# A selective-scan and expert layer on one core: a new lead-in for its first round, and its first rounds in an order written out

## Chip, cores and metric

One core of a Trainium2 chip. The time is device microseconds of one execution, the median of several runs.

## What is computed

x is 32 sequences of 256 tokens with 128 channels, fp32. First a state-space (Mamba) block on the normed x, added to x; then eight experts, two of them per token, on the normed sum, added again.

```python
xr = x @ W_in
xi, res = jnp.split(xr, 2, axis=-1)
u = silu(causal_conv4(xi) + conv_b)
dbc = u @ W_x                       # 8 columns for delta, 16 for B, 16 for C
delta = softplus(dbc_delta @ W_dt + b_dt)
h = exp(delta * A) * h + delta * B * u     # along the sequence, 256 channels x 16 states
y = (sum_n h * C + u * D) * silu(res)
x = x + y @ W_out
x = x + sum over the two best experts of p_e * (silu(n(x) @ w1[e].T) @ w2[e].T)
```

x in the first line and n(x) in the last are layer-normed over the channels.

## The kernel before

It works in 16 rounds of two sequences (512 tokens). Channels lie on partitions, so a [128, 2, 512] tile holds all 256 inner channels of a round. For each of 16 states a round has: a row of B spread over all partitions by TensorE (`row_b`, L1305, into one of two PSUM halves of `rows`), the product with `du` = delta·u on VectorE (`inputs`, L974), the decays exp(delta·A) on ScalarE (`decay`, L742), the scan on VectorE (`scan`, L984), the product with C on GpSimd (`outputs`, L471), and the sum over states as transposes that accumulate in PSUM (`sum_states`, L1326). `row_b(n)` waits for the scan of n-2, since there are two halves; `h` and `dA` are rings of eight states, so scan n waits for the sum of n-8.

Beside this, later rounds are prepared and earlier ones finished: norm (`norm_stats` L992, `inverse_deviation` L432 to L447 on GpSimd, `norm_apply` L634 on ScalarE), `turn_x`, `convolve` (L1246: the four taps times W_in as four matmuls per half, with `w_conv` made once by L1132), `conv_silu` L659, `project_bcd` L1265, `project_gate` L1256, then delta. The 8 delta columns and B must be more exact than one bf16 number: the projection is cut into high, middle and low bf16 parts (`high`, `middle`, `low`, with `take_high` and `take_middle` taking out what is already held), and `delta_rank` L1293 multiplies the parts by W_dt, split in the same way (`split_dt_weights`). softplus is relu(v) + ln(1 + exp(-|v|)): `soft_parts` L706 (abs) and L707 (relu), `soft_exponential` L715, `soft_log` L722; `add_soft` and `times_u` make `delta` and `du`. C goes through DRAM to be spread over the partitions (`store_c`, `load_c`). The experts are `hidden` (L1374, silu L776) and `expert` (L1384), weighted on VectorE (L1053) and added on GpSimd (L511).

Each engine's order is written out as one body `round_(i)` in which the parts of several rounds (i, i-1, ... i-6) are interleaved, and `run` issues it: the first bodies unrolled, the middle ones in a hardware loop, the last rounds as a list by hand. Parts of rounds that don't exist are left out, so the first bodies are the steady order with holes. Round 0's own preparation is the `lead_in` of each engine, ahead of `run`:

```python
def there(*js):
    return all(j.loop is not None or 0 <= j.at < rounds for j in js)
```

In `lead_in`, VectorE takes the statistics of round 0, copies `select`, makes `w_conv`, takes the statistics of round 1, splits W_dt and then waits for `soft_ready` to form `delta` (L1139) and `du` (L1142) of round 0. ScalarE applies the norm, copies `xnT`, does both silus, `skip`, `high`, `copy_bcd`, `middle`, `low` with the two gate silus between them, and softplus. TensorE first runs 40 transposes of the identity (L1524), then the products in that order, both gate projections and the first two rows of B. `w_bc` is filled by ten small transfers on ScalarE's queue.

## Time and profile before

| | |
|---|---|
| median of 3 runs (lowest, highest) | 1105.02 us (1104.96, 1106.01) |
| profiled execution, its span | 1103.15 us, 1101.2 us |
| TensorE (PE) busy | 1037.8 us, 94% |
| VectorE (DVE) busy | 1012.7 us, 92% |
| ScalarE (ACT) busy | 908.2 us, 82% |
| GpSimd (POOL) busy | 960.5 us, 87% |
| transfers | 76 GB/s over the span |

PEld is TensorE's weight load, which runs beside its matmuls. Times of rows are counted from the start of the span. A row of waits reads "who waited <- for whom". The granted clock of TensorE is given as a share of 2.4 GHz; it has two levels, 1.2 and 2.4 GHz.

### The profile page before, as it was taken

What the parts mean: (1) busy time and instruction counts of PE and PEld (TensorE: products, weight loads), DVE (VectorE), ACT (ScalarE), POOL (GpSimd) and SP (SyncE); (2) the same over time, 40 slices, a digit from 0 to 9 for tenths busy, and PEclk for the clock granted to TensorE, in tenths of its full rate; (3) what the DMA queues carried; (4) which work ended last, traced back from release to release, by engine and by line L of the source; (5) the groups of instructions that cost most, each with busy time, mean ns of one, the idle gap of its engine ahead of it and who ended that gap; (6) DMA issues with size and microseconds to landing.
All of it is one profiled execution on the core that took longest, in us unless ns stands there. A gap on an engine that the chain in (4) does not pass through costs nothing.

```text
span 1101.2 us, 18699 instructions
## 1 busy us (share of the span) xinstructions
PE 1037.8 (94%) x6152; PEld 759.1 (69%) x6152; DVE 1012.7 (92%) x1038; ACT 908.2 (82%) x1382; POOL 960.5 (87%) x892
## 2 busy tenths in 40 slices
PE   7558679999999999999999999999999999989997
PEld 4336457777777777767777777777777776767775
DVE  2799999999999999999999999999999999999721
ACT  4967578988999899899989999899989989875533
POOL 3388698998999999999999999999999999799834
PEclk9798889999999999999999999999999999989999
DMA  5321313104031311303131220403130120320000
GB/s 152 157 86 49 116 58 116 59 28 155 2 126 58 126 59 68 115 0 138 44 125 57 91 91 7 172 2 125 57 135 39 68 105 0 136 87 10 11 10 10
DMA packets 39760, 84.03 MB, mean 76 GB/s; under 512 B 5744, under 2 KB 30624, under 8 KB 31392
## 3 DMA queue, kind: packets, MB, share of 16 engines
q1 hardware_dynamic: 36848, 83.05, 21.0%
q10 hardware_dynamic: 2864, 0.38, 0.2%
q8 instruction: 25, 0.41, 0.2%
q14 instruction: 23, 0.19, 0.1%
HBM read 78.70 MB, written 4.72 MB: 76 GB/s over the span
## 4 chain that ended last, share of the span: by engine, by line
PE 84%; DVE 6%; ACT 4%; issue 3%; POOL 1%; DMA 0%; POOLq 0%; ACTq 0%; DVEq 0%
PE work L1384 19%; PE work L1374 18%; PE y_ps L1326 17%; PE work L1246 9%; PE rows L1305 4%; DVE h L984 4%; PE work L1265 3%; PE work L1347 3%; PE work L1230 2%; PE rows L1384 2%; PE work L1256 2%; PE rows L1374 1%; DVE rows L974 1%; PE work L1293 1%; ACT dA L742 1%
## 5 line engine op out<-in xcount | busy, mean ns | idle before, releaser
L471 POOL TENSOR_TENSOR h<-h,c_rows 128x1024 f32<-128x1024 f32 x256 | 600.4, 2367 | 75.1 <-DVE h L984 75.0
L984 DVE TENSOR_TENSOR_SCAN h<-dA,rows 128x1024 f32<-128x1024 f32 x256 | 579.4, 2276 | 1.9 <-ACT dA L742 0.7
L742 ACT ACTIVATE dA<-delta,a_neg 128x510 f32<-128x510 f32 x512 | 325.4, 708 | 1.7 <-POOL delta L455 0.5
L974 DVE TENSOR_TENSOR rows<-du,rows 128x1024 f32<-128x1024 f32 x256 | 307.1, 1213 | 3.7 <-PE rows L1305 3.6
L1326 PEld LDWEIGHTS y_ps<-ident,h 128*128 128x128 f32 x2048 | 242.6, 145 | 52.2 <-issue 36.3
L1326 PE MATMUL y_ps<-ident,h 128*128 128x128 f32 x2048 | 267.5, 278 | 2.6 <-POOL h L471 2.6
L1384 PEld LDWEIGHTS work<-w,hid 128*128 128x128 f32 x1856 | 223.2, 193 | 36.5 <-ACT hid L776 20.8
L1374 PE MATMUL work<-x2T,w 128*128 128x512 f32 x474 | 238.3, 597 | 0.3
L1384 PE MATMUL work<-w,hid 128*128 128x128 f32 x1856 | 229.0, 277 | 3.5 <-ACT hid L776 3.2
L776 ACT ACTIVATE hid<-work 128x512 f32<-128x512 f32 x237 | 139.2, 596 | 58.7 <-PE work L1374 56.8
L511 POOL TENSOR_TENSOR x<-x,weighted 128x512 f32<-128x512 f32 x128 | 163.4, 1277 | 23.4 <-DVE weighted L1053 23.0
L1305 PE MATMUL rows<-parts,select 96*128 96x512 bf16 x256 | 98.7, 387 | 32.1 <-DVE h L984 32.1
L1374 PEld LDWEIGHTS work<-x2T,w 128*128 128x128 f32 x474 | 81.9, 190 | 54.2 <-ACT hid L776 16.8
L1246 PE MATMUL work<-xnT,w_conv 128*128 128x512 f32 x256 | 116.5, 598 | 2.3 <-ACT xnT L651 1.5
L625 ACT ACT_TABLE_LOAD x73 | 93.7, 1283 | 1.3
L776 ACT ACT_TABLE_LOAD x56 | 71.8, 1283 | 22.5 <-PE work L1374 14.5
L1053 DVE TENSOR_TENSOR weighted<-work,cw 128x512 f32<-128x512 f32 x116 | 78.4, 676 | 9.3 <-PE work L1384 7.5
L1246 PEld LDWEIGHTS work<-xnT,w_conv 128*128 128x128 f32 x256 | 47.6, 191 | 51.8 <-issue 50.2
L1305 PEld LDWEIGHTS rows<-parts,select 96*128 96x128 bf16 x256 | 25.2, 99 | 65.1 <-DVE h L984 40.4
L1053 DVE TENSOR_TENSOR weighted<-rows,cw 128x512 f32<-128x512 f32 x12 | 8.2, 691 | 32.3 <-PE rows L1384 20.5
L462 POOL TENSOR_TENSOR du<-delta,u 128x1024 f32<-128x1024 f32 x15 | 35.5, 2364 | 1.8 <-POOL delta L455 1.3
L455 POOL TENSOR_TENSOR delta<-du,soft 128x1024 f32<-128x1024 f32 x15 | 35.5, 2366 | 0.0
(118 smaller groups left out, 953.9 us busy)
## 6 DMA issues: line engine op xcount, KB each, us to landing
c_rows<-c_dram SPq DMA_DIRECT2D x64, 1024.0 KB, 5.2
x_in<-in_x SPq DMA_DIRECT2D x16, 256.0 KB, 2.9
x_again<-in_x SPq DMA_DIRECT2D x16, 256.0 KB, 3.2
out<-x SPq DMA_DIRECT2D x16, 256.0 KB, 2.6
w<-in_w1T SPq DMA_DIRECT2D x1, 1024.0 KB, 6.3
w<-in_w2T SPq DMA_DIRECT2D x1, 1024.0 KB, 8.4
h<-in_conv_w SPq DMA_DIRECT2D x1, 512.0 KB, 4.9
c_dram<-bcd SPq DMA_DIRECT2D x16, 32.0 KB, 1.6
```

What stands on the lines that cost most here:

```text
L471: nc.gpsimd.tensor_tensor(at, at, c_rows[:, n, :].unsqueeze(1).broadcast_to([P, H, T]), ALU.mult).then_inc(c_used, 1)
L511: nc.gpsimd.tensor_tensor(x1[:, j.odd], x1[:, j.odd], weighted[:, e % 2], ALU.add).then_inc(expert_added, 1)
L625: nc.scalar.preload_act_table_set("natural_log_exp_and_others")
L742: last = nc.scalar.activation(two_seqs(dA[:, n % RING, half, :])[:, :, 1:], two_seqs(delta[:, half, :])[:, :, 1:], ACT.Exp, scale=a_neg[:, ...
L776: nc.scalar.activation(hid[:, e % 2, f, :], bank(place(HIDDEN, j, e, f)), ACT.Silu).then_inc(hid_ready, 1)
L974: nc.vector.tensor_tensor(rows[:, n % 2], du[:, j.odd], rows[:, n % 2, H - 1, :].unsqueeze(1).broadcast_to([P, H, T]), ALU.mult).then_inc( ...
L984: nc.vector.tensor_tensor_scan(h[:, n % RING].rearrange("p h t -> p (h t)"), dA[:, n % RING].rearrange("p h t -> p (h t)"), rows[:, n % 2] ...
L1246: last = nc.tensor.matmul(two_seqs(work[:, CONV[half], :]), w_conv[:, k, half * P:(half + 1) * P], xnT[:, :, k:k + SEQ], start=(k == 0), s ...
L1305: nc.tensor.matmul(rows[:, n % 2, H - 1, :], select[:, n, :], parts[:, j.odd, :], start=True, stop=True).then_inc(b_ready, 1)
L1326: last = nc.tensor.matmul(y_ps[:, half, b, :], h[:, n % RING, half, b * P:(b + 1) * P], ident[:, :], is_transpose=True, start=False, stop= ...
L1374: nc.tensor.matmul(bank(place(HIDDEN, j, e, f)), w1[:, e, f, :], x2T[:, j.odd, :], start=True, stop=True).then_inc(hid_projected, 1)
L1384: last = nc.tensor.matmul(token_bank(place(EXPERT, j, e))[:, b, :], hid[:, e % 2, f, b * P:(b + 1) * P], w2[:, f, e, :], start=(f == 0), s ...
```

## The change

It rewrites the lead-in of round 0 and writes out the first rounds of every engine, in place of the holed bodies:

- the first norm: VectorE aggregates and adds eps, GpSimd takes only the power, and the four 128-token blocks of `xn` are shared, two by ScalarE and two by VectorE;
- `w_conv` is made in two halves, one on VectorE, one on GpSimd;
- W_x comes with one transfer into a spare slot of `h`, and GpSimd copies its columns to their places in `w_bc` (seven copies);
- the projection of round 0 goes to another bank, starts with half 0 of `u`, and is copied whole as fp32 to `bcd`; delta's rank product is one fp32 matmul per half from these raw rows and W_dt as it is (`w_dt_first`), ahead of `high`, `middle` and `low`, which go on for B;
- softplus by halves, with the relus on VectorE; `delta` and `du` by halves;
- the gate projection, its silus and `skip` of round 0 move out of the lead-in into the first rounds;
- 27 instead of 40 transposes ahead of the first product;
- one small activation at the start loads the silu table early;
- `run` gets the index at which it begins: bodies up to 4 (TensorE, ScalarE, GpSimd), 5 (VectorE) and 6 (SyncE) are replaced by lists. The loop and the last rounds are the same.

```diff
@@ constants, helpers @@
-        WARM = 40
+        WARM = 27
+        spare = h[:, RING - 3].rearrange("p h t -> p (h t)")
+        w_dt_first = spare[0:SPLIT, 0:H * P]
+        w_x = spare[:, H * P:H * (P + RANK + 2 * NS)].rearrange("p (h n) -> p h n", h=H)
...
+            engine.tensor_tensor(w_conv[:, :, at], w_in[:, at].unsqueeze(1).broadcast_to([P, TAPS, P]),
+                                 taps_rows.rearrange("p (d k) -> p k d", k=TAPS)[:, :, at],
+                                 ALU.mult).then_inc(w_conv_ready, 1)
@@ sync @@
+                sp.wait_ge(w_dt_first_clear, 1)
+                sp.dma_start(w_dt_first[DT_ROWS[0]:DT_ROWS[0] + RANK, :], W_dt).then_inc(w_dt_first_loaded, 16)
+                fetch_x(Round(1))
                 sp.wait_ge(dt_rows_clear, 1)
...
-                fetch_x(Round(1))
...
+            sp.wait_ge(lead_norm, 1)
...
+            load_again(r[0])
+            load_again(r[1])
+            load_x(r[3])
+            load_x(r[4])
+            store_c(r[1])
+            load_c(r[1], 0)
+            load_c(r[1], 1)
+            load_x(r[5])
+            load_c(r[1], 2)
...
+            run(sp, round_, 7, 7, 19)
@@ gpsimd @@
+            pool.wait_ge(w_x_loaded, 16)
+            for half in range(H):
+                part_rows = w_bc[:, half, 0:3 * SPLIT].rearrange("p (a r) -> p a r", a=3)
+                for row, src in ((0, w_x[:, half, RANK:RANK + NS]),) + tuple(
+                        (row, w_x[:, half, 0:RANK]) for row in DT_ROWS):
+                    width = src.shape[-1]
+                    nc.gpsimd.tensor_copy(part_rows[:, :, row:row + width],
+                                          src.unsqueeze(1).broadcast_to([P, 3, width])).then_inc(w_bc_ready, 1)
+            nc.gpsimd.tensor_copy(w_bc[:, :, C_ROW:ROWS], w_x[:, :, RANK + NS:]).then_inc(w_bc_ready, 1)
+            pool.wait_ge(variance_ready[0], 1)
+            nc.gpsimd.tensor_tensor(rstd[:, 0, :], variance[:, 0, :], power[:, 0:TB],
+                                    ALU.pow).then_inc(variance_ready[0], 1)
+            pool.wait_ge(taps_loaded, 16 * TAP_LOADS)
+            weigh_taps(nc.gpsimd, 1)
...
+            inverse_deviation(r[1], 0)
+            inverse_deviation(r[2], 0)
+            outputs(r[0], 0)
+            outputs(r[0], 1)
+            outputs(r[0], 2)
+            outputs(r[0], 3)
+            outputs(r[0], 4)
+            outputs(r[0], 5)
+            inverse_deviation(r[3], 0)
...
@@ scalar @@
             act.dma_start(w_in[:, :], W_in).then_inc(taps_loaded, 16)
-            for part in range(3):
-                load(w_bc[:, :, part * SPLIT:part * SPLIT + NS],
-                     W_x[:, RANK:RANK + NS].rearrange("(h p) n -> p h n", p=P))
-            for part in range(3):
-                for row in DT_ROWS:
-                    load(w_bc[:, :, part * SPLIT + row:part * SPLIT + row + RANK],
-                         W_x[:, 0:RANK].rearrange("(h p) n -> p h n", p=P))
-            load(w_bc[:, :, C_ROW:ROWS], W_x[:, RANK + NS:RANK + 2 * NS].rearrange("(h p) n -> p h n", p=P))
...
-                pre_norm(lead)
+                act.wait_ge(constants_ready, CONSTANTS)
+                nc.scalar.activation(warm[:, :], one[:, :], ACT.Silu).then_inc(tables_warm, 1)
+                tables[0] = "silu"
+                act.wait_ge(rstd_ready[0], 1)
+                for b in range(TB // 2):
+                    last = nc.scalar.activation(xn[:, 0, b, :], x_in[:, 0, b, :], ACT.Identity,
+                                                bias=shift[:, 0, b:b + 1], scale=rstd[:, 0, b:b + 1])
+                last.then_inc(xn_ready[0], 1)
                 copy_xnT(lead)
                 act.wait_ge(weights_loaded, 16 * LOADS)
-                act.wait_ge(constants_ready, CONSTANTS)
                 for half in range(H):
                     conv_silu(lead, half)
-                skip(lead)
-                high(lead)
-                copy_bcd(lead)
-                middle(lead)
-                gate_silu(lead, 0)
-                low(lead)
-                gate_silu(lead, 1)
                 exp_tables()
-                for half in range(H):
-                    soft_parts(lead, half)
-                soft_exponential(lead)
-                soft_log(lead)
+                act.wait_ge(bcd_projected, 1)
+                nc.scalar.activation(bcd[0:ROWS, :], bcd_bank(lead)[0:ROWS], ACT.Copy).then_inc(bcd_ready, 1)
                 nc.scalar.activation(a_neg[:, :, :], a_neg[:, :, :], ACT.Exp).then_inc(a_ready, 1)
                 act.wait_ge(a_ready, 1)
                 nc.scalar.activation(a_neg[:, :, :], a_neg[:, :, :], ACT.Copy, scale=-1.0).then_inc(a_ready, 1)
                 act.wait_ge(a_ready, 2)
+                for half in range(H):
+                    act.wait_ge(dt_projected, half + 1)
+                    nc.scalar.activation(soft[:, half, :], bank(LEAD_DT[half]), ACT.Abs,
+                                         bias=dt_bias[:, half:half + 1]).then_inc(lead_abs, 1)
+                    act.wait_ge(lead_abs, half + 1)
+                    nc.scalar.activation(soft[:, half, :], soft[:, half, :], ACT.Exp,
...
+            skip(r[0])
+            decay(r[0], 0)
+            decay(r[0], 1)
+            pre_norm(r[1])
...
@@ vector @@
+            def first_norm():
+                pre_stats(r[0])
+                dve.wait_ge(stats_ready[0], 1)
+                for b in range(TB):
+                    last = nc.vector.bn_aggr(mean_variance[:, b, :], stats[:, 0, b, :])
+                last.then_inc(moments_ready[0], 3)
+                dve.wait_ge(moments_ready[0], 3)
+                nc.vector.tensor_scalar(variance[:, 0, :], mean_variance[:, :, 1], EPS, None,
+                                        ALU.add).then_inc(variance_ready[0], 1)
+                dve.wait_ge(taps_loaded, 16 * TAP_LOADS)
+                weigh_taps(nc.vector, 0)
+                dve.wait_ge(variance_ready[0], 2)
+                nc.vector.scalar_tensor_tensor(shift[:, 0, :], mean_variance[:, :, 0], -1.0, rstd[:, 0, :], ALU.mult,
+                                               ALU.mult).then_inc(rstd_ready[0], 1)
+                dve.wait_ge(rstd_ready[0], 1)
+                for b in range(TB // 2, TB):
+                    last = nc.vector.tensor_scalar(xn[:, 0, b, :], x_in[:, 0, b, :], rstd[:, 0, b:b + 1],
+                                                   shift[:, 0, b:b + 1], ALU.mult, ALU.add)
+                last.then_inc(lead_norm, 1)
+            def first_delta():
+                dve.wait_ge(weights_loaded, 16 * LOADS)
+                dve.wait_ge(bcd_ready, 1)
+                nc.vector.tensor_copy(parts[:, 0, :], bcd_bank(lead)[0:3 * SPLIT]).then_inc(high_ready, 1)
+                for half in range(H):
+                    dve.wait_ge(lead_abs, half + 1)
+                    nc.vector.tensor_scalar(du[:, 0, half, :], bank(LEAD_DT[half]), dt_bias[:, half:half + 1], 0.0,
+                                            ALU.add, ALU.max).then_inc(dt_read, 1)
+                dve.wait_ge(dt_read, H)
+                dve.wait_ge(u_ready, H)
+                for half in range(H):
+                    dve.wait_ge((lead_log, soft_ready)[half], 1)
+                    nc.vector.tensor_tensor(delta[:, half, :], du[:, 0, half, :], soft[:, half, :],
+                                            ALU.add).then_inc((lead_delta, delta_ready)[half], 1)
+                    dve.wait_ge((lead_delta, delta_ready)[half], 1)
+                    last = nc.vector.tensor_tensor(du[:, 0, half, :], delta[:, half, :], u[:, 0, half, :], ALU.mult)
+                last.then_inc(du_ready, 1)
-                pre_stats(r[0])
+                first_norm()
+                split_dt_weights()
+                pre_stats(r[1])
...
-                dve.wait_ge(rstd_ready[0], 1)
-                dve.wait_ge(taps_loaded, 16 * TAP_LOADS)
-                nc.vector.tensor_tensor(w_conv[:, :, :], w_in[:, 0:H * P].unsqueeze(1).broadcast_to(
-                    [P, TAPS, H * P]), taps_rows.rearrange("p (d k) -> p k d", k=TAPS),
-                    ALU.mult).then_inc(w_conv_ready, 1)
-                dve.wait_ge(w_conv_ready, 1)
-                pre_stats(r[1])
-                split_dt_weights()
-                dve.wait_ge(soft_ready, 1)
-                nc.vector.tensor_tensor(delta[:, :, :], du[:, 0], soft[:, :, :], ALU.add).then_inc(delta_ready, 1)
-                dve.wait_ge(delta_ready, 1)
-                dve.wait_ge(u_ready, H)
-                nc.vector.tensor_tensor(du[:, 0], delta[:, :, :], u[:, 0], ALU.mult).then_inc(du_ready, 1)
+                dve.wait_ge(w_conv_ready, H)
+                dve.wait_ge(w_bc_ready, COPIES)
+                first_delta()
+            inputs(r[0], 0)
+            inputs(r[0], 1)
+            next_pre_stats(r[2])
+            scan(r[0], 0)
+            scan(r[0], 1)
+            inputs(r[0], 2)
+            inputs(r[0], 3)
...
@@ tensor @@
                     nc.tensor.transpose(y_ps[:, 0, 0, :], ident[:, :], ident[:, :])
+                pe.wait_ge(lead_norm, 1)
                 turn_x(lead)
-                pe.wait_ge(w_conv_ready, 1)
+                pe.wait_ge(w_conv_ready, H)
                 for half in range(H):
                     convolve(lead, half, *([use_u(lead, 0)] if half and CONV[0] == CONV[1] else []))
-                pe.wait_ge(weights_loaded, 16 * LOADS)
-                project_bcd(lead)
-                project_gate(lead, 0)
+                pe.wait_ge(w_bc_ready, COPIES)
+                for half in range(H):
+                    pe.wait_ge(u_ready, half + 1)
+                    last = nc.tensor.matmul(bcd_bank(lead), w_bc[:, half, :], u[:, 0, half, :], start=(half == 0),
+                                            stop=(half == H - 1))
+                last.then_inc(bcd_projected, 1)
+                pe.wait_ge(w_dt_first_loaded, 16)
+                pe.wait_ge(bcd_ready, 1)
+                for half in range(H):
+                    nc.tensor.matmul(bank(LEAD_DT[half]), w_dt_first[:, half * P:(half + 1) * P], bcd[0:SPLIT, :],
+                                     start=True, stop=True).then_inc(dt_projected, 1)
                 take_high(lead)
-                project_gate(lead, 1)
                 take_middle(lead)
-                for half in range(H):
-                    delta_rank(lead, half, *([use_dt(lead, 0)] if half and DT[0] == DT[1] else []))
+                pe.wait_ge(dt_weights_ready, 2)
                 pe.wait_ge(select_ready, 1)
-                row_b(lead, 0)
-                row_b(lead, 1)
                 pe.wait_ge(dt_read, H)
             lead_in()
+            row_b(r[0], 0)
+            project_gate(r[0], 0, use_u(r[0], 0))
+            row_b(r[0], 1)
...
+            project_gate(r[0], 1, use_gate(r[0], 0))
+            turn_x(r[1], use_u(r[0], 1))
+            row_b(r[0], 6)
+            convolve(r[1], 0, use_gate(r[0], 1))
+            row_b(r[0], 7)
+            sum_states(r[0], 4)
+            row_b(r[0], 8)
+            sum_states(r[0], 5)
...
```

How the lists stand. **VectorE, from its statistics of round 0 to the first scan work, before:** (`BN_STATS` are the statistics, `COPY select` the rows that spread B)

```order
L1128 COPY select<-one_hot 96x2048 [waits one_hot_ready]
L1132 TENSOR_TENSOR w_conv<-w_in,h 128x1024 [waits taps_loaded,rstd_ready0]
L992 BN_STATS stats<-x_in 128x6 [waits rstd_ready0,x_loaded1,w_conv_ready]
...
L1122 TENSOR_TENSOR w_dt<-w_dt_part 96x256 [waits dt_weights_step]
L1139 TENSOR_TENSOR delta<-du,soft 128x1024 [waits soft_ready,dt_weights_ready]
L1142 TENSOR_TENSOR du<-delta,u 128x1024 [waits u_ready,delta_ready]
L992 BN_STATS stats<-x_in 128x6 [waits rstd_ready0,x_loaded0]
L992 BN_STATS stats<-x_in 128x6 x3
L974 TENSOR_TENSOR rows<-du,rows 128x1024 [waits b_ready,du_ready]
L984 SCALAR_TENSOR_TENSOR h<-dA,rows 128x1024 [waits dA_ready,b_made]
```

**and now:**

```order
L1391 BN_AGGR mean_variance<-stats 128x2 [waits stats_ready0]
L1394 TENSOR_SCALAR variance<-mean_variance 128x4 [waits moments_ready0]
L323 TENSOR_TENSOR w_conv<-w_in,h 128x4x128 [waits taps_loaded]
L1399 SCALAR_TENSOR_TENSOR shift<-mean_variance,rstd 128x4 [waits variance_ready0]
L1403 TENSOR_SCALAR xn<-x_in,rstd,shift 128x128 [waits rstd_ready0]
...
L1431 COPY select<-one_hot 96x2048 [waits one_hot_ready]
L1411 CAST parts<-rows 96x512 [waits weights_loaded,bcd_ready,w_bc_ready,w_conv_ready]
L1414 TENSOR_SCALAR du<-rows,dt_bias 128x512 [waits lead_abs] x2
L1420 TENSOR_TENSOR delta<-du,soft 128x512 [waits lead_log,u_ready,dt_read]
L1423 TENSOR_TENSOR du<-delta,u 128x512 [waits lead_delta]
L1420 TENSOR_TENSOR delta<-du,soft 128x512 [waits soft_ready]
L1423 TENSOR_TENSOR du<-delta,u 128x512 [waits delta_ready]
```

The norm's arithmetic is on VectorE, the copy of `select` and the split of W_dt stand behind it, and `delta` and `du` are made in halves.

**TensorE, from the first work of round 1 to row 7 of B of round 0, before:** (`rows<-parts,select` is a row of B, `ident,h` the sum over a state, `xnT,w_conv` a convolution half)

```order
L1230 MATMUL work<-ident,xn 128x128 [waits dt_read,xn_ready0]
...
L1246 MATMUL work<-xnT,w_conv 128x512 [waits dt_read,xnT_ready]
...
L1246 MATMUL work<-xnT,w_conv 128x512 [waits xnT_ready]
...
L1305 MATMUL rows<-parts,select 128x512 [waits scan_done] x3
L1315 MATMUL y_ps<-ident,ud 128x128 [waits skip_ready]
...
L1326 MATMUL y_ps<-ident,h 128x128 [waits c_used]
...
L1305 MATMUL rows<-parts,select 128x512 [waits scan_done] x3
L1265 MATMUL work<-u,w_bc 128x512 [waits u_ready]
```

**and now** (`xnT,w_in` is a half of the gate projection, `ident,xn` the turn of round 1):

```order
L1702 MATMUL rows<-parts,select 128x512 [waits dt_read,low_ready,select_ready,dt_weights_ready]
L1657 MATMUL work<-xnT,w_in 128x512 [waits u_ready,xnT_ready]
L1702 MATMUL rows<-parts,select 128x512
L1712 MATMUL y_ps<-ident,ud 128x128 [waits skip_ready]
...
L1702 MATMUL rows<-parts,select 128x512 [waits scan_done] x2
L1723 MATMUL y_ps<-ident,h 128x128 [waits c_used]
...
L1657 MATMUL work<-xnT,w_in 128x512 [waits gate_ready,xnT_ready]
L1631 MATMUL work<-ident,xn 128x128 [waits u_ready,xn_ready0]
...
L1702 MATMUL rows<-parts,select 128x512 [waits scan_done]
L1647 MATMUL work<-xnT,w_conv 128x512 [waits gate_ready,xnT_ready]
...
L1702 MATMUL rows<-parts,select 128x512 [waits scan_done]
L1723 MATMUL y_ps<-ident,h 128x128 [waits c_used]
...
L1647 MATMUL work<-xnT,w_conv 128x512 [waits xnT_ready]
```

From the third row of B on, the rows of round 0 stood behind both convolution halves of round 1; now seven rows stand ahead of the first half, and two between the halves.

## Rows read from the trace of the kernel before

**Rows 1.** The page's costliest groups: busy us, mean ns | idle before.
```profile
L984 DVE TENSOR_TENSOR_SCAN h<-dA,rows 128x1024 f32<-128x1024 f32 x256 | 579.4, 2276 | 1.9 <-ACT dA L742 0.7
...
L974 DVE TENSOR_TENSOR rows<-du,rows 128x1024 f32<-128x1024 f32 x256 | 307.1, 1213 | 3.7 <-PE rows L1305 3.6
```

**Rows 2.** Stretches: from:to length, busy by engine, PE clock, DMA.
```profile
36.00:60.00 24.00, 16.01 (x56) 9.74 (x57) 21.36 (x14) 19.20 (x29) 13.01 (x15) 0.85 0.09 31
60.00:120.00 60.00, 43.03 (x209) 29.46 (x209) 59.90 (x41) 40.25 (x61) 49.75 (x31) 0.86 0.17 62
120.00:182.57 62.57, 51.03 (x294) 37.17 (x292) 59.92 (x60) 51.57 (x80) 51.43 (x48) 0.92 0.25 83
182.57:247.23 64.66, 63.17 (x384) 46.20 (x384) 62.89 (x65) 57.48 (x88) 59.88 (x55) 1.00 0.21 76
...
311.04:373.81 62.77, 62.77 (x384) 46.35 (x384) 62.55 (x65) 57.49 (x88) 59.58 (x54) 1.00 0.22 79
```

**Rows 3.** DVE's waits from 36 to 247: total us, times, longest.
```profile
DVE rows L974 <- PE rows L1305: 2.2, 2, 1.8
DVE weighted L1053 <- PE work L1384: 2.0, 2, 1.0
DVE x L1024 <- PE work L1347: 1.4, 1, 1.4
DVE h L984 <- ACT dA L742: 0.7, 1, 0.7
```

**Rows 4.** Timeline of the lead-in: start us, us, engine [idle before].
```profile
4.62 0.87 DVE L992 BATCH_NORM_STATS2 stats<-x_in 128x6 f32<-128x128 f32 x4 [4.62 <-DMA x_in<-in_x]
...
8.47 1.04 POOL L444 TENSOR_TENSOR rstd<-variance,power 128x4 f32<-128x4 f32 x1
...
9.83 2.01 DVE L1132 TENSOR_TENSOR w_conv<-w_in,h 128x1024 f32<-128x1024 f32 x1 [3.21 <-POOL shift L447]
9.83 1.65 ACT L634 ACTIVATE xn<-x_in,shift,rstd 128x128 f32<-128x128 f32 x4 [2.08 <-POOL shift L447]
...
12.97 7.11 PE L1246 MATMUL work<-xnT,w_conv 128*128 128x512 f32 x16 [0.78 <-ACT xnT L651]
...
20.94 1.96 PE L1265 MATMUL work<-u,w_bc 128*128 128x512 f32 x4 [0.87 <-ACT u L659]
...
26.83 1.28 ACT L625 ACT_TABLE_LOAD   x1
...
28.12 0.69 ACT L706 ACTIVATE soft<-work,dt_bias 128x512 f32<-128x512 f32 x1
...
30.58 1.06 ACT L715 ACTIVATE soft<-soft 128x1024 f32<-128x1024 f32 x1
...
34.09 1.23 DVE L1142 TENSOR_TENSOR du<-delta,u 128x1024 f32<-128x1024 f32 x1
...
36.66 8.58 PE L1246 MATMUL work<-xnT,w_conv 128*128 128x512 f32 x16 [0.69 <-ACT xnT L651]
```

**Rows 5.** The same timeline, POOL beside DVE.
```profile
5.41 1.20 DVE L1128 COPY select<-one_hot 96x2048 bf16<-96x2048 bf16 x1
5.65 1.03 POOL L432 TENSOR_TENSOR moments<-stats 128x4 f32<-128x4 f32 x1 [1.73 <-DVE stats L992]
...
12.97 0.42 DVE L1113 TENSOR_TENSOR h<-h,w_dt_part 96x256 f32<-96x256 f32 x1
12.98 0.47 POOL L433 TENSOR_TENSOR moments<-stats 128x4 f32<-128x4 f32 x1
```

**Rows 6.** POOL's groups by line: busy us, mean ns | idle.
```profile
L511 POOL TENSOR_TENSOR x<-x,weighted 128x512 f32<-128x512 f32 x128 | 163.4, 1277 | 23.4 <-DVE weighted L1053 23.0
...
L504 POOL TENSOR_TENSOR cw<-picked 128x32 f32<-128x32 f32 x16 | 4.0, 253 | 1.3
```

**Rows 7.** DMA issues up to 60 us: KB, us to landing.
```profile
w_bc<-in_W_x ACTq DMA_DIRECT2D x4, 16.0 KB, 5.0
```

**Rows 8.** One more stretch, 36 to 158 us.
```profile
36.00:158.00 122.00, 87.84 (x413) 59.51 (x414) 117.61 (x97) 88.59 (x136) 93.20 (x68) 0.86 0.21 76
```

More of the change, by code:

```diff
@@ L424, in inverse_deviation @@
             def inverse_deviation(j, k):
-                if not there(j):
+                if not there(j) or (k == 0 and j.led()):
                     return
@@ L1297, in row_b @@
             def row_b(j, n):
-                if not there(j) or (n < 2 and j.led()):
+                if not there(j):
                     return
```

559 lines of the change are left out of this document (530 added, 29 removed).

## Prediction

> **What bounds the kernel now.** I read the costliest groups of the page first: VectorE (DVE) runs 256 scans of 2.28 us and 256 products of 1.21 us, 886.5 us of its work [rows 1]. The table of stretches then shows who sets a round's length: from 311.04 to 373.81 us, one full round, PE works 62.77 us of 62.77 and DVE 62.55 [rows 2]. TensorE (PE) and DVE both do. A round can't get shorter unless both get less to do, and the change leaves the full rounds alone. What can go is the time before the full rounds, and a microsecond won there moves all that follows: PE's remaining queue from the fourth loop body on is the same, and it has no idle time in which to lose the gain.
>
> That time has two parts. The **lead-in**: DVE writes `du` of round 0 at 34.09 for 1.23 us, so the first scan work can't begin before 35.32 [rows 4]. The **first rounds**: from 36 to 247.23 us DVE is busy 21.36, 59.90, 59.92 and 62.89 us of 24.00, 60.00, 62.57 and 64.66, which leaves 7.2 us idle [rows 2]. PE is busy only 16.01 + 43.03 of the first 84 us there. The list of waits names 6.3 of the 7.2 us: 2.2 for rows of B (PE's product stood behind both convolutions of round 1), 2.0 for experts of round 0, 1.4 for the first output projection, 0.7 for the first decays [rows 3]. No row names POOL.
>
> **The change, step by step (lead-in).**
> 1. *Norm.* DVE's statistics end at 5.49 [rows 4]. Today ten small POOL instructions follow and ScalarE (ACT) starts on `xn` at 9.83, for 1.65 us. Now DVE aggregates (4 short instructions, bounded by the 0.87 us of the four statistics; I take 0.4) and adds eps: about 6.3. POOL has to finish seven copies for `w_bc` before its power. Their source is one transfer issued at about 1.2; the nearest row needs 5.0 us to land [rows 7], so 6.2, or about 5 if it comes as soon as `x_in`, issued half a microsecond earlier and used at 4.62 [rows 4]. Seven copies at 0.25 each, as the 128x32 row [rows 6], are 1.8. I take 8.1 for the power's start (7.0 to 9.0), and 9.15 for its end (1.04, [rows 4]).
> 2. *A shared port.* The select copy on DVE ran 5.41 to 6.61, and POOL's first small instruction beside it took 1.03 us where its like take 0.2; at 12.98 another took 0.47 beside a DVE subtraction that ran to 13.39 [rows 5]. POOL waited for DVE both times. The change puts POOL's half of `w_conv` right behind the power, and DVE's `shift`, a tiny product of two SBUF operands, becomes ready at that moment. That DVE waits for POOL no row shows: 0 at one end; at the other the whole half, between 1.28 us (the 128x512 POOL sum, [rows 6]) and 2.1 (times 1.64, as DVE's `w_conv` ran 2.01 us against 1.23 for `du`). I take 0.6, less than half, since it is a race. So `shift` is there at about 10.05.
> 3. The Trainium skill (SBUF — State Buffer, section "SBUF: two separate sides") calls this pair of ports an exclusive lock: whichever instruction starts first keeps it, the other blocks for its whole length. By that the wait would be all or nothing, and the sum 0.6 us better or up to 1.5 worse; the two stretched POOL instructions agree with it for one direction.
> 4. *ACT half of `xn`*: 2 of 4 instructions, 0.9 instead of 1.65: ends 11.0 against 11.48. Turn, copy and start of the convolution then take 1.49 as today (11.48 to 12.97): it starts at 12.5. The select copy and the `dt` split leave this path for idle DVE time; if that idle time went, they would cost 1.2 + 3.3.
> 5. *Convolution and B, C*: 7.1, then silu of the second half 0.7, but the first half's product with `w_bc` already runs beside it: half of 1.96, and 0.3 of hand-over: ends at 21.6; today 22.90. The exp table load (1.28) now runs beside this, from 20.35 to 21.65, and the two gate silus (1.2) and the silu table's need for a swap at 26.83 leave the path.
> 6. *dt*: one copy to 22.25, two fp32 products (0.98 each, the first ready at 23.3), no wait for high, middle and low parts. ACT then does abs 0.69, exp, abs, exp, middle, ln, ln on 128x512 pieces. The halves of a 1.06 us exp are 0.53; with the fixed part seen in the 128x512 abs I take 0.65. First ln at 27.3, second at 27.9. The relus go to DVE beside it.
> 7. DVE: four half products of 0.64 from 27.3, the last pair after the second ln: `du` at 29.9. The low part is done at 28.5 and the row of B by 29, so they hide under it, with 1 us of cover.
>
> **Lead-in: 35.32 − 29.9 = 5.4 us gained** (3.3 to 7). The statistics of round 2 move from before the first product to behind it, which is no gain; three later ones move forward, which is no loss by 247 us.
>
> **First rounds.** The 7.2 us of idle DVE are an upper bound for what the explicit order can return. The removed waits have places: B rows 2 and 3 go ahead of everything of round 1; the convolutions stand between rows 6/7 and 8/9; the hidden products of round 0 start four rows of B earlier, which gives PE four more DVE steps for work that fills 63.17 of the last 64.66 us of this part today [rows 2]. What is late next: row 7 of B stands behind convolution half 0, half of 7.11, against a scan, a product and a scan on DVE, 5.8, before DVE needs it [rows 1]; at full clock it fits, at 1.2 GHz (twice as long) it is 1.7 us late with its neighbours, and a pair after a wait took 8.58 instead of 7.11 [rows 4]: 0 to 2 us, I take 1. The gate of round 0 now costs PE two products and ACT two silus and two table loads (3.8 us) inside round 0; ACT is busy 40.25 of the 60 us there [rows 2], so nothing; without that room round 1's parts come 3.8 late. POOL's sum and product for `du` of round 1 end when DVE reaches round 1, today without a wait that rows 3 names; 0.5. The first gating and residual sum, both earlier: 0.5. On SP, the stores and loads of C for round 1 stand behind two loads of x that wait for norms of rounds 1 and 2; those end before the C of round 1 is computed, since its convolution needs the first of them: nothing, and if they are late POOL's outputs wait, with eight states of `h` as cover. **7.2 − 2.0 = 5.2 us gained** (2 to 7.2).
>
> **Sum**: 10.6 us. The profiled execution took 1103.15 us, so 1092.5; the median of the runs shown is 1.87 above it, so **1094.4 us**. A measurement of this kernel can tell about 0.2% (2.2 us) from no change.
>
> **Rivals** (times against the median).
> - *B, everything returns*: no new waits and an early `shift`: 6.5 + 7 = 13.5, 1091.5. For it: PE is idle a third of the first rounds. Against: `du` of round 1 comes with no spare time. 0.15.
> - *C, only the lead-in*: the explicit order trades its 7.2 us of waits for others of the same size. For it: from 36 to 120 us the PE clock is granted at 0.85 and 0.86 of full speed [rows 2], so work that fits at full clock may not. 1099.6. 0.17.
> - *D, the port lock in full*: POOL's half goes first and takes 2.1 us: 1.5 more than in the sum, 1095.9. It is the page's rule above; rows 5 bear out one direction. 0.15.
> - *E, no change*: the change doesn't do what it says. The first row of B still waits for all split parts and the split `dt` weights; round 1's `du` still goes through POOL. If either chain is some 8 to 10 us late, all is given back: 1104. Against: DVE reaches the split by 11 us and has until 28.5 for it. 0.04.
> - *F, slower: TensorE at its lower clock*. From 36 to 158 us PE is busy 87.84 us of 122.00 at a mean granted clock of 0.86 [rows 8]: 28% of it at 1.2 GHz, the rest at 2.4. With busy time spread evenly that is 75.5 us of work at full clock. The new order puts nearly every product of rounds 0 and 1 behind a wait for a scan. If the part s of the work runs at 1.2 GHz it takes 75.5(1+s); it limits DVE (117.61 busy) from s = 0.56, and loses to today's 122 + 5.4 from s = 0.69; at 0.8 it takes 136, that is 8.5 us slower, 1113.5. Against: s was about 0.28 with the same waits, and PE's amount of work per DVE step hardly moves. 0.03. The Trainium skill (TensorE: Matmul & The Clock Gate, "HAM oscillation — how this bites in real kernels") warns of just this, matmul groups split by waits that each start cold; the 8.58 us row agrees for one group.
>
> **Chances.** The forecast has 0.46; its own range is 1091.5 to 1097.5. With the fast end of B and most of C, the range is **1090.5 to 1100.0**; outside lie E, F and tails. Faster by over 0.2%: 0.93; within: 0.04; slower: 0.03.
>
> **What the profile would show.** First product of DVE at 28.5 to 31.5 instead of 36.01; POOL's power over by 10; the convolution starting between 11.5 and 13.5; `shift` right behind the power, or only behind POOL's half (D). DVE idle from its first product to the fifth loop body 1 to 4 us instead of 7.2, waiting for B rows near the first convolution of round 1. Granted clock near 0.85 to that point. Full rounds of 62.8 us as before. Wrong would be: DVE idle for `du` of round 1, a PE mean clock near 0.6, or full rounds that grow.

## The result, and the profile after

The changed kernel takes 1099.36 us (median of 4 runs, 1098.39 to 1100.40) against 1104.99 for the kernel before in the same comparison: ratio 0.9944, 95% interval 0.9929 to 0.9959. That is 5.6 us less, where 10.6 were forecast. The profiled execution took 1100.40 us with a span of 1098.4; before it was 1103.15 and 1101.2. Between the two profiles lie only 2.75 us, and the first thing to do is to say where those are.

Table of stretches of the changed kernel, from VectorE's first product to the start of the fifth loop body (its third output projection), then two full rounds, then the next one. Columns as in [rows 2].
```profile
32.30:243.00 210.70, 179.22 (x944) 124.17 (x943) 204.26 (x180) 173.61 (x263) 173.83 (x146) 0.90 0.22 77
243.00:369.60 126.60, 125.95 (x766) 92.48 (x765) 125.33 (x129) 115.05 (x175) 118.60 (x108) 1.00 0.22 79
369.60:433.30 63.70, 63.05 (x384) 46.19 (x382) 62.70 (x65) 57.86 (x89) 60.93 (x56) 1.00 0.23 83
```
Before, the same stretches run from 36.01 to 247.10 (211.09 us, DVE busy 203.91), to 373.70 (126.60), and to 436.80 (63.10). So the first product is 3.7 us earlier, the fifth body 4.1 us, and the seventh still 4.1. Then gain is lost: the round from 369.60 takes 63.70 instead of 63.10, with PE busy 63.05 against 63.01. The sixteenth output projection starts at 1048.3 against 1051.1: 2.8 us are left.

Timeline of the changed kernel's lead-in: start, us, engine [idle before].
```profile
8.21 1.03 POOL L478 TENSOR_TENSOR rstd<-variance,power 128x4 f32<-128x4 f32 x1
9.23 1.51 POOL L323 TENSOR_TENSOR w_conv<-w_in,h 128x512 f32<-128x512 f32 x1
9.28 1.48 DVE L1399 SCALAR_TENSOR_TENSOR shift<-mean_variance,rstd 128x4 f32<-128x4 f32 x1 [2.02 <-POOL rstd L478]
...
11.81 0.63 PE L1631 MATMUL work<-ident,xn 128*128 128x128 f32 x4 [4.09 <-ACT xn L952]
...
13.22 8.62 PE L1647 MATMUL work<-xnT,w_conv 128*128 128x512 f32 x16 [0.78 <-ACT xnT L766]
...
32.30 2.36 DVE L1235 TENSOR_TENSOR rows<-du,rows 128x1024 f32<-128x1024 f32 x2
```
The norm is on time (power from 8.21, forecast 8.1). Then `shift`, a 4-column product, takes 1.48 us: it ends with GpSimd's half of `w_conv`. TensorE, idle for 4.09 us before the turn of `xn`, then needs 8.62 us for the convolution instead of 7.11 [rows 4]. The granted clock over it is 0.82, so part of it ran at 1.2 GHz; before it was 1.00. The stretches of the two convolutions, first the changed kernel's, then the one before (columns as in [rows 2]):
```profile
13.22:21.84 8.62, 8.62 (x17) 3.90 (x18) 3.26 (x10) 0.69 (x1) 3.64 (x10) 0.82 0.25 89
```
```profile
12.97:20.08 7.11, 7.10 (x16) 2.90 (x16) 2.80 (x9) 1.97 (x2) 3.33 (x10) 1.00 0.41 156
```

What VectorE waited for between 32 and 243 us (total, times, longest):
```profile
DVE rows L1235 <- PE rows L1702: 2.9, 4, 1.4
DVE weighted L1314 <- PE work L1781: 1.5, 2, 1.0
DVE yT L1276 <- PE work L1631: 1.2, 1, 1.2
DVE x L1285 <- PE work L1744: 0.2, 1, 0.2
```
The waits for decays, output projection and experts of [rows 3] are gone or smaller, and new ones stand in their place: `yT` for the turned y of round 0 (1.20), and for rows of B 2.9 us in all instead of 2.2, the longest for row 13 of round 1 behind the second convolution half of round 3 (1.39). Idle in all: 6.4 us against 7.2.

ScalarE's timeline in the round that grew, 416 to 425 us:
```profile
416.74 1.28 ACT L740 ACT_TABLE_LOAD   x1
418.03 1.95 ACT L856 ACTIVATE dA<-delta,a_neg 128x510 f32<-128x510 f32 x3
421.21 1.94 ACT L856 ACTIVATE dA<-delta,a_neg 128x510 f32<-128x510 f32 x3 [1.23 <-issue]
423.17 1.28 ACT L890 ACT_TABLE_LOAD   x1
```
The same place in the kernel before:
```profile
420.81 1.28 ACT L625 ACT_TABLE_LOAD   x1
422.11 3.78 ACT L742 ACTIVATE dA<-delta,a_neg 128x510 f32<-128x510 f32 x6
426.57 1.28 ACT L776 ACT_TABLE_LOAD   x1 [0.68 <-PE work L1384]
```
Six decays ran in one piece before; now ScalarE stops for 1.23 us between the two halves of one state, where the program has no wait. Before, ScalarE even had 0.68 us to spare behind them. It stops behind the same activation three times more, until 547.54 (for 0.97), 673.82 (0.99) and 799.85 (0.75). The place can be read from the program: the loop's body ends with `decay(one, 7)` and begins with `decay(two, 8)`, so the third activation of the row at 418.03 is the first of a new pass. The loop holds two rounds and runs five passes; the four stops stand one activation behind its four returns to the start, and there is none where it is entered or left. TensorE then waits for `hid`:
```profile
425.12 2.05 PE L1781 MATMUL work<-w,hid 128*128 128x128 f32 x16 [0.66 <-ACT hid L890]
```
The list of DMA queues names a candidate. From 430 to 830 us the changed kernel has the row below; the kernel before has no instruction queue in that stretch at all.
```profile
q14 instruction: 15, 0.12, 0.1%
```
Over the whole execution it is 43 packets against 23.

### The profile page after: what moved, and what is told of

Its sections match the earlier page's. It is cut to its first block, busy times and chain, and to the rows that moved or that the text cites. A ratio compares the mean times of both kernels' runs of the same rounds, so it can differ in the third digit from the quotient of the medians.

```text
span 1098.4 us, 18682 instructions
## 1 busy us (share of the span) xinstructions
PE 1042.4 (95%) x6139; PEld 758.1 (69%) x6139; DVE 1016.4 (93%) x1051; ACT 907.8 (83%) x1381; POOL 961.4 (88%) x892
## 4 chain that ended last, share of the span: by engine, by line
PE 74%; DVE 8%; issue 7%; ACT 6%; POOL 4%; DMA 0%; POOLq 0%; ACTq 0%; DVEq 0%
PE work L1781 17%; PE work L1771 16%; PE y_ps L1723 16%; PE work L1647 8%; DVE h L1245 6%; PE rows L1702 4%; PE work L1744 2%; ACT dA L856 2%; PE work L1631 2%; PE work L1666 2%; PE rows L1781 2%; POOL h L535 2%; PE work L1657 2%; PE rows L1771 1%; DVE rows L1235 1%
## 5 line engine op out<-in xcount | busy, mean ns | idle before, releaser
L1723 PE MATMUL y_ps<-ident,h 128*128 128x128 f32 x2048 | 270.8, 279 | 10.9 <-POOL h L535 10.9
L774 ACT ACTIVATE u<-work,conv_bias 128x512 f32<-128x512 f32 x32 | 22.0, 687 | 16.5 <-PE work L1647 16.3
```

Of the source, the lines that this page charges most:

```text
L1723: last = nc.tensor.matmul(y_ps[:, half, b, :], h[:, n % RING, half, b * P:(b + 1) * P], ident[:, :], is_transpose=True, start=False, stop= ...
```

## Experiments

Three theories for the missing five microseconds: the **port** (GpSimd holds up VectorE's `shift`), the **cold start** (TensorE partly at 1.2 GHz in the first convolution, since it had idled), and **code** (ScalarE's loop is loaded anew in each pass, since its place in the program has moved). Their common rival is that the first rounds have a limit of their own and swallow whatever the lead-in gains. First product, fifth body and idle VectorE between them are read from each profile; "full rounds" is from the third to the fourteenth output projection, eleven rounds.

| kernel | us, ratio to before (95%) | first product | fifth body | idle DVE | full rounds |
|---|---|---|---|---|---|
| before (profile) | 1103.15 | 36.01 | 247.1 | 7.2 | 694.1 |
| changed | 1099.36, 0.9944 (0.9929 to 0.9959) | 32.30 | 243.0 | 6.4 | 695.5 |
| e1_port | 1099.12, 0.9938 (0.9925 to 0.9950) | 32.15 | 242.8 | 6.5 | 695.9 |
| e2_warm | 1098.07, 0.9930 (0.9917 to 0.9943) | 32.46 | 240.5 | 4.3 | 695.7 |
| e3_pad | 1098.17, 0.9931 (0.9919 to 0.9944) | 33.89 | 242.6 | 5.0 | 694.2 |
| e4_three | 1095.83, 0.9911 (0.9898 to 0.9925) | 30.52 | 240.8 | 6.4 | 694.3 |
| e8_pad6 | 1099.25, 0.9936 (0.9922 to 0.9949) | 33.98 | 242.5 | 4.7 | 694.2 |
| h1_old_lead_new_order | 1102.73, 0.9974 (0.9965 to 0.9982) | 37.11 | 247.4 | 6.2 | 694.1 |
| h2_new_lead_old_order | 1109.04, 1.0035 (1.0022 to 1.0048) | 34.08 | 252.6 | 14.5 | 694.1 |
| e5_after_shift | 1097.54, 0.9934 (0.9921 to 0.9947) | 32.05 | 240.1 | 4.3 | 694.1 |
| e6_order | 1096.68, 0.9919 (0.9907 to 0.9932) | 33.65 | 241.3 | 3.9 | 694.2 |
| e7_all | 1094.32, 0.9892 (0.9877 to 0.9907) | 29.74 | 237.2 | 3.7 | 694.2 |
| before_again | 1103.12 (one) | 36.08 | 247.1 | 7.1 | 694.1 |
| before_warm46 | 1106.07, 0.9998 (0.9988 to 1.0008) | 36.07 | 248.9 | 8.9 | 694.1 |

Below the changed kernel (before: 1104.99) the medians belong to four comparisons, in which the kernel before took 1105.92, 1105.86, 1106.99 and 1105.77; so kernels of different comparisons are compared by their ratios.

**e1_port**
```diff
-            pool.wait_ge(taps_loaded, 16 * TAP_LOADS)
-            weigh_taps(nc.gpsimd, 1)
                 weigh_taps(nc.vector, 0)
+                weigh_taps(nc.vector, 1)
```


> The changed kernel, but VectorE makes both halves of w_conv while it waits for the power anyway, and GpSimd makes none. Port theory (VectorE's shift took 1.48 us because GpSimd's half of w_conv held the shared port from 9.23 to 10.74): shift takes about 0.2 us and is there at 9.5 instead of 10.76, xn and the convolution start 1.3 us earlier (near 11.9 instead of 13.22), the first product of VectorE comes 1.0 to 1.3 us earlier, and the time falls by about that, 1098.1. Rival (shift waited for the result of the power or for something else, as a semaphore that arrives late): shift stays at 1.4 us and nothing moves.

`shift` took 0.16 us instead of 1.48: the wait was GpSimd's half of `w_conv`. But it began only at 10.43, since the two pieces on VectorE now held up GpSimd:
```profile
6.44 2.13 DVE L323 TENSOR_TENSOR w_conv<-w_in,h 128x512 f32<-128x512 f32 x2 [0.22 <-DMA h<-in_conv_w]
...
6.80 2.43 POOL L474 COPY w_bc<-h 128x48 f32<-128x48 f32 x6 [3.66 <-DMA h<-in_W_x]
```
The copies took 1.48 us in the changed kernel. The theory holds, the edit only turned the wait round: first product 0.15 us earlier, time unchanged where 1.3 us less was expected.

**e2_warm**
```diff
-        WARM = 27
+        WARM = 40
```


> The changed kernel with 40 warming transposes instead of 27, so that TensorE is busy until about 10.7 and idle for 1.1 us instead of 4.1 before the turn of xn. Cold theory (the first convolution took 8.62 us instead of 7.11 because TensorE had idled and began at 1.2 GHz): it takes 7.1 to 7.3 us, the products behind it 0.1 less, and all behind comes 1.5 us earlier: 1097.9. Rival (the convolution is slow because of weights or data, or the gain is lost in the first rounds): 8.6 us, or the first product earlier by 1.5 with the body marks unmoved.

Missed. The 40 transposes took 6.30 us, not 7.46 as in the kernel before, and ended at 9.50; after 2.28 us of idle time the convolution took 8.80. The fifth body still came 2.5 us earlier, with the first product where it was: from it to the fifth body the mean granted clock was 0.94 instead of 0.90, and the waits for rows of B at 146, 160 and 187 us were gone. With the same order and the same first product, the first rounds thus differ by 2.2 us of idle VectorE together with the granted clock; what moved the clock is not shown. The difference to e1_port (0.9930 against 0.9938) is within the intervals.

**e3_pad** and **e8_pad6** (with 6)
```diff
+                for k in range(12):
+                    nc.scalar.activation(warm[:, :], one[:, :], ACT.Silu).then_inc(tables_warm, 1)
+                    act.wait_ge(tables_warm, k + 1)
                 nc.scalar.activation(warm[:, :], one[:, :], ACT.Silu).then_inc(tables_warm, 1)
```


> The changed kernel with 12 more tiny activations at the start of ScalarE's program, in time that it idles (3.4 to 10.8 us). In the changed kernel ScalarE stops for 1.23, 0.97, 0.99 and 0.75 us in every second full round with no releaser, while an instruction queue (q14) loads 5 packets in each 126 us pass of the loop; before, it loaded none between 420 and 840 us. Code theory (ScalarE's loop no longer stays loaded since its place in the program moved by the 10 to 12 instructions that its lead-in lost): with 12 put back these loads and stops go, full rounds are 62.8 to 63.1 again as before, and the time falls by the 1.3 to 1.4 us that the marks lost between 370 and 690 us. Rival (it depends on something else, as the phase of the engines or on VectorE's program): stops and loads stay, no difference.

> The changed kernel with 6 tiny activations instead of 12, so that ScalarE's loop begins 6 instructions further on than in the changed kernel and 6 short of e3_pad. Code theory (it is a question of place alone): either no loads in the loop and no stops, as in e3_pad, or both as in the changed kernel, and not half of each; 23 packets on q14 or 43. If it were the time that the tiny activations take or warm something, half the stops would be left.

Both show the code theory right, with nothing in between: 23 packets on the queue, none of them from 430 to 830 us, no stop. ScalarE at the same place in e3_pad:
```profile
416.39 1.28 ACT L740 ACT_TABLE_LOAD   x1
417.69 3.78 ACT L856 ACTIVATE dA<-delta,a_neg 128x510 f32<-128x510 f32 x6
422.15 1.28 ACT L890 ACT_TABLE_LOAD   x1 [0.68 <-PE work L1784]
```
The column of full rounds has two groups only: 695.5 to 695.9 in the three kernels that load in the loop, 694.1 to 694.3 in all others. A few instructions that do nothing are worth 1.3 to 1.8 us there. In the traces 448 ScalarE instructions stand ahead of its loop in the changed kernel, 457 in the one before (the ten loads of `w_bc` became one); with 6 more, 454, it already stays loaded. In the whole time the gain is not clear of noise (0.9931 and 0.9936 against 0.9944, intervals overlap); in both profiles TensorE started cold and slower (convolution 9.54 and 9.73, first product 1.6 and 1.7 later). That this lateness comes from the added instructions is not shown; e6_order has it too, e5_after_shift and e7_all do not.

**e4_three**: e1, e3 and WARM = 38.

> The three edits together (both halves of w_conv on VectorE; 38 warming transposes; 12 more tiny activations). If the three theories hold and the costs add: 1.3 + 1.5 + 1.4 = 4.2 us less than the changed kernel, 1095.2. If the first rounds have a limit of their own (TensorE or the chain of rows of B), the first product is near 29.6 but the marks of the loop bodies gain only a part of 2.7 us.

Here the warming held: after 1.94 us of idle time the convolution took 7.11 us at full clock, and the first product came at 30.52. The time fell nearly as expected (0.9911; 3.6 us less than the changed kernel by the ratios, 4.2 forecast). The 1.8 us won in the lead-in are still there at the fifth body, 2.1 us earlier, so the first rounds did not swallow them.

**h1_old_lead_new_order** (the diff: the kernel before, `run(pe, round_, 4, 16)` and its like on the other queues replaced by the lists of the changed kernel and `run(pe, round_, 5, 4, 16)`) and **h2_new_lead_old_order**:
```diff
+            row_b(lead, 0)
+            row_b(lead, 1)
+            run(pe, round_, 0, 4, 16)
...
+            skip(lead)
+            run(act, round_, 0, 4, 16)
```


> The kernel before with its own lead-in, and with the first rounds of all five queues in the explicit order of the changed kernel (what its lead-in has done already is skipped: the gate, the skip term and the first two rows of B of round 0). In the comparison of the two profiles the first rounds went from 7.2 to 6.4 us of idle VectorE. If the order is worth that (0 to 1 us), the first product stays at 36.0 and the fifth loop body begins at 246 to 247 us: 1 us or less below the kernel before. If the order is worth the 5.2 us of the prediction and the new lead-in spoils them: about 242 and 5 us less.

> The changed kernel with its new lead-in, and with the first rounds in the old order (the loop's body with holes, as before; the first two rows of B, and the skip term, right behind the lead-in; the gate of round 0 in its loop body), and 10 more tiny activations so that ScalarE's loop stands where it did before. If the lead-in is the whole gain: the first product near 32.3 and the fifth body at 243.4, 3.7 us earlier than before, and 3.7 us less time than before. If the gate's products in round 0 need the new order, rows of B wait longer than 1.84 us near 42 us, and less than 3 us of the gain is left.

h2 also has 10 more tiny activations, so that ScalarE's loop stays loaded. These two are the largest surprise. The order alone gives 0.9974, 2.9 us. The new lead-in alone makes the kernel slower than before, 1.0035, and its fifth body is 5.5 us later. One wait does it, at the first scan (0.7 before, [rows 3]):
```profile
43.90 2.29 DVE L1032 TENSOR_TENSOR_SCAN h<-dA,rows 128x1024 f32<-128x1024 f32 x1 [8.60 <-ACT dA L776]
```
and ScalarE's timeline there says why:
```profile
32.74 1.28 ACT L703 ACT_TABLE_LOAD   x1
34.40 0.60 ACT L703 ACTIVATE gate<-work 128x512 f32<-128x512 f32 x1 [0.37 <-PE work L1336]
37.22 0.60 ACT L703 ACTIVATE gate<-work 128x512 f32<-128x512 f32 x1 [2.23 <-PE work L1336]
37.72 1.64 ACT L669 ACTIVATE xn<-x_in,shift,rstd 128x128 f32<-128x128 f32 x4
40.56 0.60 ACT L686 ACTIVATE xnT<-work 128x512 f32<-128x512 f32 x1 [1.20 <-PE work L1310]
41.17 1.28 ACT L660 ACT_TABLE_LOAD   x1
42.47 7.44 ACT L776 ACTIVATE dA<-delta,a_neg 128x510 f32<-128x510 f32 x12
```
The lead-in is shorter because the gate of round 0 has left it. In the old order the gate, with two table loads and two waits for TensorE, comes to stand ahead of the first decays. The explicit order puts decays ahead of it; that is its first use.

**e5_after_shift**: e3_pad, and `pool.wait_ge(rstd_ready[0], 1)` ahead of GpSimd's half.

> The changed kernel with the 12 tiny activations of e3_pad, and GpSimd's half of w_conv put behind VectorE's shift by a wait. In e1_port shift took 0.16 us, but came only 0.3 us earlier, since two halves of w_conv on VectorE held up GpSimd's copies and power by 1.1 us. Port theory: with one half on VectorE the power ends at 9.25, shift at about 9.45, GpSimd's half by 11.1, before the convolution needs it, and the convolution starts near 11.9, 1.3 us earlier; 1.3 us less than e3_pad at the same TensorE clock. Rival: the half of w_conv on GpSimd holds up VectorE's part of xn instead (1 us), and the convolution starts at 12.7 or later.

The rival was right, and by more: `shift` took 0.16 us at 9.28, then
```profile
9.48 1.80 DVE L1407 TENSOR_SCALAR xn<-x_in,rstd,shift 128x128 f32<-128x128 f32 x2
9.59 1.61 POOL L323 TENSOR_TENSOR w_conv<-w_in,h 128x512 f32<-128x512 f32 x1 [0.34 <-DVE shift L1403]
```
The wait moved by one instruction; `xn` took 0.60 elsewhere. The time is no less than that of e3_pad (0.9934 against 0.9931), where 1.3 us less was expected.

**e6_order**: e3_pad with two moves on TensorE.
```diff
+            turn_y(r[0], 1, use_u(r[2], 0))
             sum_states(r[1], 0)
             sum_states(r[1], 1)
-            turn_y(r[0], 1, use_u(r[2], 0))
...
+            row_b(r[1], 13)
             score(r[0], use_x2T(r[0]))
-            row_b(r[1], 13)
```


> The changed kernel with the 12 tiny activations of e3_pad and two steps moved in TensorE's order: the second half of turn_y of round 0 ahead of two sums of states of round 1, and row 13 of B of round 1 ahead of the scores of round 0. VectorE waits 1.20 us for the one and 1.39 (2.09) for the other in all profiles of the new order. If these waits are due to what stands ahead on TensorE: 1.2 and 0.9 us less, the fifth body begins 2 us sooner than with e3_pad and the time is 2 us less. If others take their place (VectorE runs into the wait for experts of 0.99 anyway): less than 1 us.

Idle VectorE 3.9 us against 5.0. The wait for `yT` went and one of 0.66 for a row of B came; row 13 was waited for 1.59 instead of 2.09. So 1.1 us, between the two expectations; the time does not tell it from e3_pad (0.9919 against 0.9931, intervals overlap).

**e7_all**: the 12 activations, WARM = 42, `pool.wait_ge(lead_norm, 1)` ahead of GpSimd's half, and the moves of e6_order.

> The changed kernel with everything that the runs so far point to: 12 tiny activations (ScalarE's loop where it stood), GpSimd's half of w_conv behind VectorE's part of xn, 42 warming transposes, and the two moved steps of e6_order. In e5_after_shift the half of w_conv behind shift stretched VectorE's part of xn from 0.60 to 1.80 us; behind xn nothing is in its way. Port theory: shift at 9.4, xn by 10.3, the turn of xn near 10.5 and the convolution near 11.8, at full clock 7.1 us; first product near 29.0. With 1.3 (port) + 1.5 (clock) less than e6_order (1096.7): 1093.9. If the turn waits for the transposes, or the gain is lost to waits of the first rounds: 1095 to 1096.

```profile
9.55 0.16 DVE L1403 SCALAR_TENSOR_TENSOR shift<-mean_variance,rstd 128x4 f32<-128x4 f32 x1 [2.02 <-POOL rstd L478]
...
10.77 0.63 PE L1635 MATMUL work<-ident,xn 128*128 128x128 f32 x4 [0.71 <-ACT xn L956]
...
12.17 7.11 PE L1651 MATMUL work<-xnT,w_conv 128*128 128x512 f32 x16 [0.78 <-ACT xnT L767]
...
29.74 2.36 DVE L1239 TENSOR_TENSOR rows<-du,rows 128x1024 f32<-128x1024 f32 x2
```
0.9892: the fastest of all, its interval below that of the changed kernel. First product 29.74, fifth body 237.2, 9.8 us earlier than before. GpSimd's half of `w_conv` now held up VectorE's subtraction at 10.58 (1.71 us, elsewhere 0.42) and nothing that the first product needed.

**before_again** and **before_warm46** (WARM = 46) ask why the median fell by 5.6 us and the profile by 2.75.

> The kernel before once more, for a second profile. The profile shown of it belongs to one of its shortest executions (1103.15; median 1105 to 1106), and h1_old_lead_new_order, which has the same lead-in, had its first convolution at 8.80 us and its first product at 37.1 instead of 36.0. If this is what the shown profile missed, an ordinary execution of the kernel before has a convolution of about 8.6 to 8.8 us or a lower granted clock up to 158 us than 0.86, and the first product later by 1 us or the fifth body later than 247.1. If the spread lies elsewhere: the same lead-in and marks, and a difference in the full rounds.

> The kernel before with 46 warming transposes instead of 40, and nothing else. Its profile is the same to 0.1 us each time it is taken (1103.15, 1103.12, first convolution at full clock, 7.11 us), but its other executions take 1105 to 1107. h1_old_lead_new_order has the same lead-in and 8.80 us there. If the other executions begin the first convolution at the lower clock: with 46, TensorE idles for less than 1.2 us before the turn of xn, the convolution is at full clock each time, and the median falls by 1 to 2 us (ratio 0.998 to 0.999), near the profile's 1103. If the spread lies elsewhere: the same ratio to the kernel before, 1.000, and 1105 to 1107.

The profile of the kernel before repeated to 0.1 us, and more warming changed nothing (0.9998), so a cold first convolution is not what makes its other executions longer. But the profile of before_warm46 belongs to an ordinary execution (1105.13) and has the same lead-in up to the first product. It parts from [rows 4] at the convolution of round 1, 9.62 us instead of 8.58, and at the row of B behind it:
```profile
46.58 1.23 DVE L974 TENSOR_TENSOR rows<-du,rows 128x1024 f32<-128x1024 f32 x1 [2.88 <-PE rows L1305]
```
Idle VectorE to the fifth body is then 8.9 us, not 7.2, and the fifth body comes at 248.9. The granted clock from the first product to the fifth body is 0.91 instead of 0.92, and apart from six transposes the two programs are the same, so TensorE's clock in the first rounds is the likely cause. That most executions of the kernel before are of this kind is likely but rests on one profile.

## Why the prediction was half right

The direction and the range (1090.5 to 1100.0) held; of the gain a half was there. That the time came near rival C (1099.6) is partly luck: C's reason, waits traded for others of the same size, fits the two profiles (7.2 us idle against 6.4), but its price takes the lead-in's 5.4 us as won, and 3.05 were. Of the signs that the prediction named, the power (over at 9.24) and the convolution's start (13.22) came true. The first product (32.30, not 28.5 to 31.5) and idle VectorE (6.4, not 1 to 4) did not, and full rounds that grow were named as a sign of being wrong.

Counted from the end of `du` as in the prediction (35.32 before, 32.27 now), the lead-in gave 3.05 of 5.4 us, the first rounds 1.0 of 5.2, and the full rounds took 1.4.

- **Norm and power** (8.1 forecast): 8.21. Right.
- **The port** (0.6 us in the sum, up to 2.1): 1.3. This was rival D: the race was lost, since `shift` and GpSimd's half become free in the same moment, and GpSimd, which is there already, began 0.05 us earlier. Three runs show that it goes both ways: `shift` 1.48 to 0.16 (e1), GpSimd's copies 1.48 to 2.43 (e1), `xn` 0.60 to 1.80 (e5), and VectorE's subtraction 0.42 to 1.71 (e7). The Trainium skill (SBUF — State Buffer, section "SBUF: two separate sides") says that whichever starts first keeps the pair for the whole instruction; these rows agree (`shift` ended at 10.76, GpSimd's half at 10.74), and none shows the halfway value of the sum.
- **Convolution** ("start as today", 7.1): 8.62. This step failed. I took 7.11 from [rows 4] and did not ask what TensorE does ahead of it: 27 transposes end at 7.73, and 4.09 us of idle time follow. The price was in the same view, 8.58 for the convolution of round 1. In the profiles with 0.7 to 1.9 us of idle time ahead of the turn (before, before_again, before_warm46, e4, e7) the convolution took 7.11, in those with 2.3 to 4.1 (all others) 8.62 to 9.73. The number of transposes alone does not decide it: with 40 it took 8.80 in e2, and 8.80 in h1, which has the old lead-in.
- **From the B and C rows to `du`**: forecast 8.3 us (21.6 to 29.9), measured 8.5 (23.74 to 32.27). Right. The convolution started 0.7 us late by the port and took 1.5 longer: the two steps above are nearly all of the lead-in's error. In e7, without them, the first product came at 29.74.
- **First rounds** (5.2 us back): 0.4 us from first product to fifth body in the shown pair. This step failed by its size: "a removed wait has a place" is true, but two new ones of 1.2 and 1.4 us came with the order, and TensorE's mean clock there fell from 0.92 to 0.90. By the medians the order is worth more, 2.9 us (h1); in the profile of h1 the first product is 1.1 us later than before and the fifth body 0.3, so there it gave 0.8.
- **The gate costs nothing in round 0**: true only in the new order; in the old one its cost was 8.60 us at one wait (h2). The cover that I named, ScalarE's idle time, was the wrong one: the gate's place against the first decays decides.
- **"No idle time in which to lose the gain"**: failed. PE's queue was full, but each pass of the loop got a stop on ScalarE, 1.4 us in all. Nothing in the diff of the loop could show it, as the loop was not changed.

The account of the two profiles, counted from the first product: 3.7 (lead-in) + 0.4 (first rounds) − 1.4 (code) = 2.7 of 2.75 us. The other 2.9 of the median's 5.6 are 1.84, by which the shown profile of before was below its median in the comparison, and 1.04, by which that of the changed kernel was above. Of the first, before_warm46 shows a likely cause; the cause of the second is open.

## What to carry to other kernels

A lead-in and the order of what follows it are one edit: a step that leaves the lead-in must have its new place ahead of nothing that the first loop steps wait for. When code is added or taken away ahead of a hardware loop, compare the start times of the loop's bodies and the instruction queues' packets too, even if the loop is untouched; a few idle instructions may put it back. Where GpSimd and VectorE held each other up, as here, GpSimd's work is better started behind the small VectorE steps of the critical chain than beside them, and warming should reach up to the first product that it is for.

## What the runs showed of the hardware

- ScalarE's loop of two rounds either stays loaded (no packet on its instruction queue from 430 to 830 us) or loads anew in each pass (15 packets), decided by 6 instructions ahead of it. In the kernels that reload, ScalarE stopped for 0.75 to 1.26 us one activation behind each of the loop's four returns to its start.
- Some pairs of a VectorE and a GpSimd instruction exclude each other here: VectorE's `shift`, fp32 `xn` and subtraction against GpSimd's product for `w_conv`, and GpSimd's copies against VectorE's products for `w_conv`. Others do not: `xn` at 10.79 took its 0.60 us beside GpSimd's selects of `one_hot` (10.70, 0.95), and a bf16 product on VectorE took 0.29 at 15.69 beside GpSimd's power (15.47, 1.08, the kernel before). VectorE's scans and products, which read one operand from PSUM, take 2.28 and 1.21 us in the mean over all 256, with GpSimd's 256 products of 2.37 us running in the same rounds.
- A profile can be an exact repeat of itself (1103.15 and 1103.12) and still not be an ordinary execution of its kernel (median 1105 to 1107).
